# Scan stage of a Mamba layer: the mix of gathered expert rows moves from VectorE to ScalarE and GpSimd

## What is computed

```python
x = _layernorm(x + _L1_ffn_ref(x, ...), axis=-1)    # mixture of experts, the 4 best of 32 experts a token
x = _layernorm(x + _L2_attn_ref(x, ...), axis=-1)   # the scan

# _L2_attn_ref, for every item
x_bld, z_bld = jnp.split(hidden_states @ in_proj_w.T, 2, axis=-1)
xc = silu(causal_conv4(x) + conv_b)                 # 512 channels
dt_lo, Bm, Cm = split(x_ld @ x_proj_w.T)
delta = jax.nn.softplus(dt_lo @ dt_proj_w.T + dt_proj_b)
def step(h, inp):                                   # 512 channels x 16 states, over 256 tokens
    dA = jnp.exp(d_t[:, :, None] * negA[None])
    h = dA * h + (d_t * x_t)[:, :, None] * B_t[:, None, :]
    y_t = jnp.einsum('bdn,bn->bd', h, C_t)
y = (y + x_ld * D) * silu(z_bld)
out = y @ out_proj_w.T
```

## Time and profile before

| | us |
|---|---|
| median of 3 runs | 2512.0 (2511.66 to 2514.43) |
| the profiled execution | 2519.74 |
| its span, first to last instruction | 2518.0 |
| TensorE busy | 2217.8 (88%) |
| VectorE busy | 1674.2 (66%) |
| ScalarE busy | 1453.1 (58%) |
| GpSimd busy | 889.7 (35%) |
| scan of step 0, item 0, to the last scan's start | 1255.3 to 1756.3 |

### The profile page before, as it was taken

How to read it: one execution, slowest core, us unless ns; L and a number is a source line. 1 busy time by engine, 2 the same in 40 slices (tenths; PEclk the granted TensorE clock), 3 DMA queues, 4 the chain that set the end, 5 groups by cost and what they waited for, 6 DMA issues and landing times. The chain is left out here.

```text
span 2518.0 us, 47690 instructions
## 1 busy us (share of the span) xinstructions
PE 2217.8 (88%) x16425; PEld 1937.2 (77%) x16425; DVE 1674.2 (66%) x4020; ACT 1453.1 (58%) x3815; POOL 889.7 (35%) x906
## 2 busy tenths in 40 slices
PE   6887979999999979998489999999686899996997
PEld 4776968999999959997266676677685576766997
DVE  5785767888888846554498898777464554554554
ACT  5674547777777723333487777775342566663342
POOL 3221240011111120000678887667485233332000
PEclk8897989999999979999699999999897999997999
DMA  4000120000000463333311111000400000000001
GB/s 151 1 1 17 35 68 18 2 18 18 18 18 18 144 197 119 120 111 94 129 41 51 51 50 47 35 35 1 119 1 1 1 1 1 1 1 1 1 1 34
DMA packets 74371, 111.77 MB, mean 44 GB/s; under 512 B 16174, under 2 KB 59814, under 8 KB 73016
## 3 DMA queue, kind: packets, MB, share of 16 engines
q1 hardware_dynamic: 66648, 87.23, 10.7%
q0 software_dynamic: 7488, 21.50, 2.6%
HBM read 79.73 MB, written 28.97 MB: 43 GB/s over the span
## 5 line engine op out<-in xcount | busy, mean ns | idle before, releaser
L2064 POOL TENSOR_TENSOR l2a_hb<-l2a_hb,l2a_Cb 128x1024 f32<-128x1024 f32 x128 | 302.8, 2377 | 107.7 <-DVE l2a_hb L2551 106.5
L2551 DVE TENSOR_TENSOR_SCAN l2a_hb<-l2a_dA,l2a_dB 128x1024 f32<-128x1024 f32 x128 | 288.8, 2275 | 31.4 <-PE l2a_dB L2158 26.1
L2158 PE MATMUL l2a_dB<-l2a_diag,l2a_dxT 64*128 64x128 f32 x2048 | 190.1, 306 | 38.8 <-DVE l2a_hb L2551 25.9
L2158 PEld LDWEIGHTS l2a_dB<-l2a_diag,l2a_dxT 64*128 64x128 f32 x2048 | 139.9, 194 | 104.0 <-PE l2a_dB L2158 37.2
L2388 ACT ACTIVATE l2a_dA<-l2a_delta,l2a_An 128x255 f32<-128x255 f32 x512 | 213.4, 498 | 6.9 <-DVE l2a_hb L2551 6.7
L964 PE MATMUL l1a_QK<-l1a_xh,early_wqkv_h 128*128 128x256 f32 x512 | 147.1, 287 | 1.5 <-DVE l1a_xl L128 1.5
L964 PE MATMUL l1a_QK<-l1a_xh,early_wqkv 128*128 128x256 f32 x512 | 144.6, 282 | 0.0
L964 PE MATMUL l1a_QK<-l1a_xl,early_wqkv_h 128*128 128x256 f32 x512 | 144.3, 282 | 0.0
L2178 PE MATMUL l2a_YS<-ident,l2a_hb 128*128 128x128 f32 x1024 | 142.2, 285 | 1.0 <-POOL l2a_hb L2064 1.0
L1240 ACT ACTIVATE l1a_ex<-l1a_S,l1a_nm 128x256 f32<-128x256 f32 x256 | 119.3, 471 | 36.5 <-DVE l1a_nm L1292 35.1
L2178 PEld LDWEIGHTS l2a_YS<-ident,l2a_hb 128*128 128x128 f32 x1024 | 116.5, 145 | 12.2 <-POOL l2a_hb L2064 1.3
(11 more groups left out here) (767 smaller groups left out, 7812.4 us busy)
## 6 DMA issues: line engine op xcount, KB each, us to landing
l2a_Cb<-c_rows SPq DMA_DIRECT2D x8, 2048.0 KB
l1f_xl<-moe_x_rows SPq DMA_DIRECT2D x95, 128.0 KB
moe_y_rows<-l1f_yo SPq DMA_DIRECT2D x95, 128.0 KB, 1.7
first_raw<-in_L_attn_w_qkv_dram SPq DMA_DIRECT2D x18, 256.0 KB, 2.8
moe_x_rows<-X SPq DMA_DIRECT2D x1, 4224.0 KB, 17.2
l1f_dL<-in_L_ffn_Wd_dram SPq DMA_DIRECT2D x1, 3072.0 KB
X<-in_L_attn_x_dram SPq DMA_DIRECT2D x8, 256.0 KB, 6.0
routes_raw<-in_L_attn_w_o_dram SPq DMA_DIRECT2D x4, 512.0 KB
```

Of the source, the lines that this page charges most:

```text
L2064: nc.gpsimd.tensor_tensor(h[:, :, :], h[:, :, :], Cb[p][:, s0:s0 + UN, :], ALU.mult).then_inc(hc_ready, 1)
L2158: last = nc.tensor.matmul(out[:, m:m + 2, j * P + a:j * P + a + HP], dxT[q][a:a + HP, j, c * P:(c + 1) * P], diag[q][a:a + HP, j, s0 + m:s ...
L2551: nc.vector.tensor_tensor_scan(flat(hb[u % RING]), flat(dA[(i * NU + u) % DAS]), dB[u % 2][:, :], 0.0, ALU.mult, ALU.add).then_inc(scanned, 1)
```

## The change

- ScalarE scales the gathered rows in place, in steps 10 and 11, four operations of 128x256 a half (`act_scale`).
- GpSimd adds them up in steps 11 and 12 (`pool_mix`): rows 0 and 1 with rows 2 and 3 (128x512), the two sums (128x256), and the residual (128x256).
- VectorE keeps the statistics (`dve_mix_stats`), now behind the scan of step 13.
- GpSimd's `pool_rstd` goes from step 8 to step 14, ScalarE's `act_mixed` from step 12 to step 15.
- The first half's gathers go from steps 5, 6, 13, 14 to steps 12 to 15.
- Items 0 to 2, whose mixes are made ahead of the scans, are mixed as before.

```diff
-    SECOND_HALF, FIRST_HALF = (0, 1, 2, 3), (5, 6, 13, 14)
-    MIX = {3: (0, (0, 1)), 4: (0, (2, 3)), 5: (1, (0, 1)), 6: (1, (2, 3))}
+    SECOND_HALF, FIRST_HALF = (0, 1, 2, 3), (12, 13, 14, 15)
+    SCALE_AT, ADD_AT, STATS_AT, MIXED_AT = 10, 11, 13, 15
...
+        def pool_mix(pool, k, j):
+
+            pool.wait_ge(m_scaled, ((k - 3) * NT + j + 1) * TOPK)
+            nc.gpsimd.tensor_tensor(my[j][:, 0:2, :], my[j][:, 0:2, :], my[j][:, 2:4, :], ALU.add).then_inc(m_summed, 1)
+            if j == 0:
+                pool.wait_ge(m_done, k * NT)
+            pool.wait_ge(m_summed, (k * NT + j) * TOPK + 1)
+            nc.gpsimd.tensor_tensor(mr[:, j, :], my[j][:, 0, :], my[j][:, 1, :], ALU.add).then_inc(m_summed, 1)
+            pool.wait_ge(m_summed, (k * NT + j) * TOPK + 2)
+            nc.gpsimd.tensor_tensor(mr[:, j, :], mr[:, j, :], sh.X[:, k, j], ALU.add).then_inc(m_summed, 2)
...
+                    if u in (ADD_AT, ADD_AT + 1) and i + 3 < ITEMS:
+                        pool_mix(pool, i + 3, u - ADD_AT)
+                    if u == STATS_AT + 1 and i + 3 < ITEMS:
+                        pool_rstd(pool, i + 3)
                     if u in SECOND_HALF and not first and i + 3 < ITEMS:
                         pool_gather(pool, i + 3, 1, SECOND_HALF.index(u))
                     if u in FIRST_HALF and i + 4 < ITEMS:
                         pool_gather(pool, i + 4, 0, FIRST_HALF.index(u))
-                    if u == 8 and i + 3 < ITEMS:
-                        pool_rstd(pool, i + 3)
...
+        def act_scale(act, k, j):
+
+            act.wait_ge(half_in[j], 16 * TOPK * (k - 1))
+            for n in range(TOPK):
+                nc.scalar.activation(my[j][:, n, :], my[j][:, n, :], ACT.Copy,
+                                     scale=sh.moe_wk[:, k * NT + j, n:n + 1]).then_inc(m_scaled, 1)
...
-                    if u == 12 and i + 3 < ITEMS:
+                    if u in (SCALE_AT, SCALE_AT + 1) and i + 3 < ITEMS:
+                        act_scale(act, i + 3, u - SCALE_AT)
+                    if u == MIXED_AT and i + 3 < ITEMS:
                         act_mixed(act, i + 3)
                     if u == 14 and ahead:
                         act_keep_dx(act, k, q)
...
+        def dve_mix_stats(dve, k):
+
+            for h in range(NT):
+                dve.wait_ge(m_summed, (k * NT + h + 1) * TOPK)
+                nc.vector.bn_stats(m_st[:, h, :], mr[:, h, :]).then_inc(m_stats_ready, 1)
+            dve.wait_ge(m_stats_ready, (k + 1) * NT)
+            nc.vector.memset(ph.carrier[:, :], 0.0)
+            for h in range(NT):
+                nc.vector.bn_aggr(m_mv[:, h, :], m_st[:, h, :]).then_inc(m_var_ready, 1)
...
-                    if u in MIX and i + 3 < ITEMS:
-                        dve_mix(dve, i + 3, *MIX[u])
+                    if u == STATS_AT and i + 3 < ITEMS:
+                        dve_mix_stats(dve, i + 3)
```

More of the change, by code:

```diff
@@ L1913, in l2_attn @@
                                       for k, n in enumerate(("shift_ready", "m_shift_ready")))
+        m_scaled = ctx.enter_context(nc.semaphore("l2a_m_scaled", num=PHASE_SEMS.stop + 7))
         wi_loaded = ctx.enter_context(nc.semaphore("l2a_wi_loaded", num=POOL_DMA_SEMS.stop))
@@ L2496, in dve_mix @@
                                                ).then_inc(m_summed, 1)
[L2497 to L2504, removed]
+            if j == NT - 1:
+                dve_mix_stats(dve, k)
+        def dve_mix_stats(dve, k):
[6 more added lines that the diff above has]
+                nc.vector.bn_aggr(m_mv[:, h, :], m_st[:, h, :]).then_inc(m_var_ready, 1)
         def dve_dx(dve, q):
```

## The result

| | before | after |
|---|---|---|
| median of 4 runs each, us | 2511.84 (2511.66 to 2514.43) | 2556.83 (2553.24 to 2558.2) |
| ratio | | 1.0174 (1.0157 to 1.0192) |
| profiled execution, us | 2519.74 | 2555.98 |

A forecast was written before the change was run, and what follows sets the result against it. TensorE was taken to pace steps 0 to 7, GpSimd's queue to decide the boundary. Item delays of 41.8 us plus 1 for the clock, 42.8 on a 2512.0 us median, gave 2555 us; range 2531 to 2568.

The forecast's parts named there:

- In steps 0 to 7 TensorE sets the pace and the mix on VectorE is hidden already: Steps 0 to 7: 32.78 us with or without a mix, so taking it off VectorE gains 0.
- that 0: Item 0, steps 0 to 9: the change makes this stretch no longer or shorter, 0 us.
- The first wait: Behind scan 13 VectorE waits 7.6 us for GpSimd's second half; TensorE's step 0 products start 3.7 us later.
- The second wait: At the boundary ScalarE's tap stands behind act_mixed, which waits for GpSimd's norm; products of step 3 start 8.5 us later.
- the step 6 of the forecast: GpSimd's queue, some 8 us late at step 0 of the next item, catches up by step 6.
- The items apart: Loss by item at the boundaries: item 0 9.6 us, items 1 to 3 8.5 each, item 4 6.7; sum 41.8.
- Item 4's discount for its missing gathers: Item 4's boundary: 2.5 us fewer gathers, but multiply 14 waits for scan 14, so 1.8 less: 6.7 us.
- The clock: New TensorE idling near boundaries brings 1.2 GHz windows, mostly while it waits: 1 us in all, upper bound 3 an item.
- Only the direct stall counts: Rival at the boundary: only step 0's products wait for scan 14, 3.7 us for five items, 2531 us; chance 0.13.
- The faster rival: Second half added before scan 13 ends, nothing waits; ScalarE's step 12 gains 0.8 us an item, 2508 us; chance 0.05.
- The clock or the adds make it worse: Rival: TensorE idling brings one or two more half-rate windows an item, 8 to 16 us more, 2563 to 2571; chance 0.17.

The follow-up runs named there:

- the first experiment: Changed kernel with ScalarE's norm act_mixed moved from step 15 to step 1 of the next item, behind both taps: 2538.2 us, ratio 1.0123.
- the second: Changed kernel with GpSimd's six adds an item cut to two elements a row: 2541.6 us, ratio 1.0129.
- the fifth run: Kernel before with only ScalarE's act_mixed moved from step 12 to step 1 of the next item: 2507.1 us, ratio 0.9988.
- the fourth run: Changed kernel's three-engine mix moved to other steps: scalings 3 and 6, adds 4 and 6, statistics 7, ScalarE's norm 12: 2511.2 us, ratio 1.0010.

## Why the prediction was right

**What bounds the stage.** "In steps 0 to 7 TensorE sets the pace and the mix on VectorE is hidden already": shown by the kernel that keeps the new assignment in other steps (500.94 us for 500.95). It holds for items 1 to 6, which all took 32.78 us before, with a mix or without. In item 0 VectorE was the pace, and the mix did cost 4.8 us up to scan 7. The forecast didn't look at this stretch; that 0 came out right for its steps 0 to 9 is luck, as the waits ahead of scans 8 and 9 take all but 0.3 us of it back.

**The first wait.** VectorE stands 7.6 us behind scan 13, the 7.6 of the forecast. Scan 14 starts 30.98 us after scan 7, forecast 30.65. The adds are 0.73 and 1.29 us each, as taken; a half occupies 2.99 us, not 2.75, since each of the two dependent adds starts 0.14 us behind the end of the one before it (1376.22 + 1.29 to 1377.65). That is the 0.3 us. The 0.95 us of statistics before, from 1414.59 on, are 1.03 in the trace; the 0.7 that the sum used measured 0.63 (1384.51 to 1385.14).

**The second wait.** ScalarE stands 8.60 us ahead of the norm, the convolution starts 40.79 us after scan 7 (forecast 40.45), scan 0 of the next item 43.14 (42.8), the products of step 3 49.98 (49.75). GpSimd catches up sooner than the step 6 of the forecast: its multiply of step 0 of item 2 waits for its scan again (1.85 us), as the scans are late too. Taking the norm away from the tap gave back 18.5 us of the stage; taking both waits away 33 of 44.

**The items apart.** 9.84, 8.76, 10.39, 7.76 and 6.90 against 9.6, three times 8.5, and 6.7. The 10.39 holds the window of item 3 (1.65), the 7.76 the 1 us by which that item was longer before. Item 4's discount for its missing gathers was right in size, and the run with the gathers elsewhere shows its mechanism, multiply 14 waiting for its scan.

**The clock.** I put 1 us in for it, "mostly in time in which TensorE waits anyway". For the changed kernel that holds: there is a window at each of the five boundaries, which the wait for VectorE covers, one that isn't covered (1.65 us, item 3), and 0.5 us at item 5. Where the uncovered ones fall was not forecast. They came to 1.65 us and twice 0.5, less the 1 us that item 3 had lost to its own before, so 1.6 in all; that this is near the 1 us is in part luck. The step was wrong as soon as I used it for the experiments. In the first I left it out and was 7 us off: there the window at the boundary lies on the chain, 1.6 us in three of the four items from scan 7 to scan 7. In the second it came in the next stretch, 1.65 us in three items, two more than in the changed kernel.

**The rivals.** "Only the direct stall counts", 2531 us, fell: it is in substance the first experiment, and gave 2538 with the tap freed. The faster rival fell with it. Its gain of 0.8 us an item is real where the norm leaves ScalarE's step 12 and nothing else is lost, as the fifth run shows. "The clock or the adds make it worse", 2563 to 2571, fell as well: the adds took 0.24 us a half more than I had, and of the new windows one alone fell into steps 0 to 7 of an item. That VectorE is freed of the mix, and of standing still in it while GpSimd multiplies, brought nothing, as the fourth run shows.

## What to carry to other kernels

Before work is moved from a busy engine to idle ones, compare a stretch with the work and one without it: here both last 32.78 us, and so the move could gain nothing there. What counts is not the engine but the step in which the last consumer stands: an in-order queue that waits for a product passes its wait on to all that is behind it, and with a 1 us norm taken away from ahead of a tap the stage was 18.5 us shorter, with 4 us an item of adds taken away 17.4. The added work belongs where the engine that sets the pace covers it. Where it can't stand there, its consumers belong far behind it: put into the next item they gave back 33 of the 44 us.

## What the runs showed of the hardware

- A window of TensorE at 1.2 GHz cost 1.6 to 1.7 us where TensorE was the chain and nothing where it waited right afterwards: 16 sums took 3.62 us in the changed kernel and 3.49 in the first experiment, in place of 1.91, and only the second was longer for it (71.14 us an item; 69.45 where the sums took 1.91). Shortening a wait can turn the one into the other.
- VectorE's eight weighted adds of 2 elements a row kept most of their busy time beside GpSimd's multiplies (8.19 us, with 256 elements 9.64). The Trainium skill (SBUF — State Buffer, "Who interferes with whom") has two such instructions exclude each other for a whole instruction. The trace agrees, and shows more: an add that started during the first of two multiplies in a row ended behind the second, 2.8 us after its start. A busy share of VectorE that contains such operations is not work that could be saved by making them smaller.
- An add on GpSimd that waits for the add before it started 0.14 us behind its end (0.08 in one place, 1382.80 to 1382.88), where independent operations overlap by 0.05.
